# Graph-network layer: gathers as copies with POOL adding them, count blocks copied two units at a time, 92 instead of 100 counted rows

## The reference, cut to what is computed

```python
msg = x[src] + edge_attr                      # 400000 x 64
agg = segment_sum(msg, dst, 12500)
h = relu(agg @ W1 + b1)                       # 64 -> 128
y = x + h @ W2 + b2                           # 128 -> 64
out = (y - mean(y)) / sqrt(var(y) + 1e-5)
```

## Time and profile before

| | us |
|---|---|
| median of 3 runs | 1739.51 (1737.26 to 1742.28) |
| the profiled execution's own time | 1733.04 |
| its span, first to last instruction | 1731.1 |
| PE busy | 1445.1 (83%) |
| DVE busy | 1404.8 (81%) |
| ACT busy | 1182.7 (68%) |
| POOL busy | 1053.7 (61%) |

### The profile page before, as it was taken

The page is one execution under the profiler, slowest core; times in us unless marked ns, Lnnn a source line. Parts: engine busy times, 40 slices in busy tenths (PEclk is TensorE's granted clock), DMA queues, the critical chain, the costliest instruction groups (busy, mean ns, idle before and its releaser), DMA issues.

```text
span 1731.1 us, 49895 instructions
## 1 busy us (share of the span) xinstructions
PE 1445.1 (83%) x19203; PEld 1248.4 (72%) x19204; DVE 1404.8 (81%) x2881; ACT 1182.7 (68%) x2314; POOL 1053.7 (61%) x749
## 2 busy tenths in 40 slices
PE   1357777878998988899999999999999888899884
PEld 1246666767887878888888888888887766777653
DVE  5499999989999899998888888888898666766343
...
GB/s 170 138 81 98 100 100 110 97 91 98 103 103 95 98 88 100 106 100 92 88 87 94 93 86 84 100 82 91 86 87 74 79 57 65 57 54 50 14 66 70
DMA packets 219371, 152.99 MB, mean 88 GB/s; under 512 B 128167, under 2 KB 218039, under 8 KB 218791
## 3 DMA queue, kind: packets, MB, share of 16 engines
...
## 4 chain that ended last, share of the span: by engine, by line
PE 42%; DVE 23%; issue 13%; ACT 13%; DVEq 4%; POOL 1%; POOLq 0%; another core or an unknown queue 0%
PE sums_ps L1132 18%; PE counted_ps L1116 14%; ACT counts L724 12%; DVE oh_key L918 9%; DVE oh_lo L914 8%; PE chunk_ps L1100 6%; DVE onehot L875 3%; DVEq L888 2%; PE turn_ps L1144 2%; DVE lists L896 1%; DVE less_b L827 1%; POOL x_parts L642 1%; DVEq L896 1%; PE turn_ps L1072 0%; PE counted_ps L1203 0%
## 5 line engine op out<-in xcount | busy, mean ns | idle before, releaser
L724 ACT CAST counts<-counted_ps 128x392 bf16<-128x392 f32 (+2 forms) x2018 | 1039.5, 607 | 351.8 <-PE counted_ps L1116 295.2
L601 POOL DMA_INDIRECT gmsg<-in_x,idx_t x625 | 965.0, 1544 | 207.8 <-issue 189.9
L1116 PE MATMUL counted_ps<-oh_key,oh_lo 128*128 128x98 bf16 (+2 forms) x5903 | 756.9, 235 | 162.0 <-DVE oh_key L918 89.8
L1132 PE MATMUL sums_ps<-x_parts,counts 128*128 128x193 bf16 (+3 forms) x6272 | 801.7, 251 | 0.1
L1116 PEld LDWEIGHTS counted_ps<-oh_key,oh_lo 128*128 128x128 bf16 x5903 | 427.5, 100 | 300.5 <-DVE oh_key L918 130.2
L1132 PEld LDWEIGHTS sums_ps<-x_parts,counts 128*128 128x128 bf16 (+3 forms) x6272 | 601.2, 120 | 6.9 <-issue 1.1
L914 DVE TENSOR_TENSOR oh_lo<-counted_ps,tables 128x768 bf16<-128x768 f16 (+5 forms) x773 | 508.1, 657 | 102.4 <-PE counted_ps L1116 94.4
L918 DVE TENSOR_TENSOR oh_key<-counted_ps,tables 128x1176 bf16<-128x1176 f16 (+3 forms) x773 | 572.2, 740 | 0.0
L610 POOL DMA_INDIRECT records<-edge_records,run_at x47 | 49.1, 1045 | 363.8 <-DVE run_at L832 362.9
L1100 PE MATMUL chunk_ps<-onehot,cmsg 128*64 128x32 f32 (+1 forms) x5000 | 188.6, 231 | 25.5 <-DVE lists L896 17.3
L1100 PEld LDWEIGHTS chunk_ps<-onehot,cmsg 128*64 128x64 f32 x5000 | 172.7, 146 | 44.5 <-DVE lists L896 25.7
...
## 6 DMA issues: line engine op xcount, KB each, us to landing
cmsg<-in_edge_attr SPq DMA_DIRECT2D x500, 160.0 KB
gmsg<-in_edge_attr SPq DMA_DIRECT2D x125, 160.0 KB
gmsg<-in_x,idx_t POOLq DMA_INDIRECT x625
...
```

The source lines that it names most:

```text
L601: pool.indirect_dma_start(gmsg[:, at * D:(at + 1) * D], None, x, bass.IndirectOffsetOnAxis(ap=idx_t[:, of:of + 1], axis=0), compute_op=ALU ...
L724: nc.scalar.copy(to, ps.rearrange("p (n h) -> p h n", h=HI)).then_inc(unit_kept, 1)
L1116: mm = nc.tensor.matmul(unit_ps[u % BANKS][:, col:col + slot.key_cols], oh_lo[s % RING][:, n * P:(n + 1) * P], oh_key[s % RING][:, n * slo ...
L1132: mm = nc.tensor.matmul(sums_ps[0:n, 0:XC], counts[b % 2][:, h * P:h * P + n], x_parts[:, h * XC:(h + 1) * XC], start=(h == 0), stop=(h == ...
```

## The change

1. Eight rows of five chunks move from counted to gathered: 460 counted and 165 gathered chunks. The plan has 1609 units, 671 slots, 54 blocks and 43 groups instead of 2018, 773, 64 and 47; what goes are the last 102 slots, all of width three.
2. A gather is a plain copy into a tile of its own, `xmsg` (four buffers). Before gather n POOL waits until gather n - 2 has landed. A POOL instruction (`mix`) adds the 128x320 chunk to the edge features in `gmsg`; that of chunk k - 1 stands after the third gather of chunk k. PE waits for the mix, not the gathers. `gmsg` has six buffers instead of ten.
3. Two units of equal size in one block are copied by one ACT instruction (815 copies). They lie in two neighbouring PSUM banks, and two such pairs of banks take turns. The constants that DVE compares with move to another bank, and the products of both pairs of a quad share one bank.
4. The three parts of a block's sums are added by DVE (`add_parts`: a copy and two adds of 64 columns, each waiting for the one before) and no longer by PE. ACT copies the degree column alone. PE turns them with one matmul.
5. The time scale: 7.35 us per gathered chunk instead of 9.4, and a gathered pair is due two chunks later after its gathers than before.

```diff
-CROWS = 100
+CROWS = 92
...
-    FIRST, LAST = 45.0, 20.0 + 9.4 * gathered + 1.4 * groups
+    FIRST, LAST = 45.0, 20.0 + 7.35 * gathered + 1.4 * groups
...
-    pairs = [(20.0 + chunk * (k + 2) + 5.0, "gather", k) for k in range(0, gathered - 1, 2)]
+    pairs = [(20.0 + chunk * (k + 4) + 4.0, "gather", k) for k in range(0, gathered - 1, 2)]
...
-    BANKS = 3
+    EVICTED = []
+    for u, unit in enumerate(UNITS):
+        if EVICTED and len(EVICTED[-1]) == 1 and (UNITS[u - 1].block, UNITS[u - 1].nodes) == (unit.block, unit.nodes):
+            EVICTED[-1].append(u)
+        else:
+            EVICTED.append([u])
...
-    GSLOTS, CSLOTS = 10, 6
+    GSLOTS, XSLOTS, CSLOTS = 6, 4, 6
...
+        ADD_PARTS.setdefault(min(s0 + n + 2, NS), []).append(b)
+        to = min(s0 + n + 3, NS)
...
             def gather(k, j):
-                t = k % GSLOTS
-                if j == 0:
-                    pool.wait_ge(gin[t], 16 * (k // GSLOTS + 1))
+                t = k % XSLOTS
+                if k >= XSLOTS and j == 0:
+                    pool.wait_ge(mixed, (k - XSLOTS + 1))
                 at, of = t * TILES + j, k * TILES + j
-                pool.indirect_dma_start(gmsg[:, at * D:(at + 1) * D], None, x,
-                                        bass.IndirectOffsetOnAxis(ap=idx_t[:, of:of + 1], axis=0),
-                                        compute_op=ALU.add).then_inc(gathered[t], 16)
+                if of >= 2:
+                    landed(of - 2)
+                pool.indirect_dma_start(xmsg[:, at * D:(at + 1) * D], None, x,
+                                        bass.IndirectOffsetOnAxis(ap=idx_t[:, of:of + 1], axis=0)
+                                        ).then_inc(gathered[of % 4], 16)
+
+            def mix(k):
+                s, t = k % GSLOTS, k % XSLOTS
+                pool.wait_ge(gin[s], 16 * (k // GSLOTS + 1))
...
+                to = gmsg[:, s * TILES * D:(s + 1) * TILES * D]
+                nc.gpsimd.tensor_tensor(to, to, xmsg[:, t * TILES * D:(t + 1) * TILES * D], ALU.add).then_inc(mixed, 1)
...
-                nc.scalar.copy(to, ps.rearrange("p (n h) -> p h n", h=HI)).then_inc(unit_kept, 1)
+                nc.scalar.copy(to.rearrange("p h (m n) -> p h m n", m=m),
+                               ps.rearrange("p m (n h) -> p h m n", h=HI)).then_inc(unit_kept, 1)
...
-                nc.scalar.copy(sums[0:n, 0:XC - 1], sums_ps[0:n, 0:XC - 1]).then_inc(sums_copied, 1)
+                nc.scalar.copy(degrees[0:n, b:b + 1], sums_ps[0:n, XC - 1:XC]).then_inc(degrees_kept, 1)
...
+            def add_parts(b):
+                n = BLOCK_ROWS[b]
+                part = lambda k: sums_ps[0:n, k * D:(k + 1) * D]
+                dve.wait_ge(block_summed, b + 1)
+                dve.wait_ge(degrees_kept, b + 1)
+                if b:
+                    dve.wait_ge(sums_turned, b)
+                nc.vector.tensor_copy(sums[0:n, :], part(0)).then_inc(parts_added, 1)
+                dve.wait_ge(parts_added, 2 * b + 1)
+                nc.vector.tensor_tensor(sums[0:n, :], sums[0:n, :], part(1), ALU.add).then_inc(parts_added, 1)
+                dve.wait_ge(parts_added, 2 * b + 2)
+                nc.vector.tensor_tensor(sums[0:n, :], sums[0:n, :], part(2), ALU.add).then_inc(sums_copied, 1)
...
-                if piece.opens and u >= BANKS:
-                    pe.wait_ge(unit_kept, u - BANKS + 1)
...
+                eviction, bank = EVICTION[u]
+                if piece.opens and not bank and eviction >= 2:
+                    pe.wait_ge(unit_kept, eviction - 1)
...
-                for k in range(PARTS):
-                    mm = nc.tensor.matmul(turn_ps[0:D, 256:256 + n], sums[0:n, k * D:(k + 1) * D], ident[0:n, 0:n],
-                                          start=(k == 0), stop=(k == PARTS - 1))
-                mm.then_inc(sums_turned, 1)
+                nc.tensor.matmul(turn_ps[0:D, 256:256 + n], sums[0:n, :], ident[0:n, 0:n], start=True, stop=True).then_inc(sums_turned, 1)
```

107 lines of the change are left out of this document (62 added, 45 removed).

## The result

The changed kernel takes 1800.59 us (median, 1797.9 to 1821.53) against 1739.51: ratio 1.0372, 95% interval 1.0269 to 1.0474. Forecast were 1548 us and a range to 1620. The profiled execution is the slowest of the three, 21 us above the median: 1821.53 us, its span is 1819.4. First the page's busy times, its clock row, and the chain.

A forecast was written before the change was run, and what follows sets the result against it. DVE bounded width one, PE width two, ACT width three; POOL had room. 1733 - 235 + 30 + 15 - 9 + 10 (both lines ending together) + 2 (chunks behind the last slot) = 1546, predicted 1548 us, range 1505 to 1620.

The forecast's parts named there:

- The 102 slots, -235: Last stretch of width three, from 1387 on: its count matmuls, copies and block multiplies go, saving 235 us; tail unchanged.
- Sums, +15: Block sums on DVE: +17 at width one, +6 at width two, -8 for PE's fewer products; together +15 us.
- chunks moved, +30: 17 quads spread over earlier slots: 9 at 2.1 us where DVE limits, 8 at 1.36 where PE does; +30 us.
- PE's relief: Width two: PE loses two of three fp32 products per block, 16 us for 28 blocks; half counted, -8 us.
- Copies, -9: ACT's copy of two units taken as 0.75 us; pays in the 30 remaining slots of width three, -9 us.
- the rival of the banks: PE waits for ACT to free double banks; 0.15 us for each of 448 pairs is +67, 1615 us; chance 0.1.
- POOL, 8.0 us a chunk: Five gathers, two in flight, plus the mix take POOL 8.0 us (7.2 to 9.2); POOL ends at 1415.
- the prediction's own five steps: POOL's time for a chunk's five gathers and mix; a 3.1 us landing gives 8.2 us, 3.6 gives 9.2.
- Slower than before: The wait for the gather two back makes the kernel slower above 9.3 us a chunk, landing about 3.65; chance 0.04.
- the formula: Total time when POOL limits: 91 + 159 chunks at c us each + 52 for record loads + 107 behind.
- the hold-up between POOL's adds and DVE: Rival: each of 165 mixes stops DVE for 0.7 us, up to +116, 1664 us; chance 0.06.
- POOL's pace: Rival: landings of 3.3 us or more make chunks 8.6 to 9.2 us, total 1617 to 1713; chance 0.17.

The follow-up runs named there:

- e1: Changed kernel with the old adding gathers (ten buffers, no wait on one another), old time scale and 100 counted rows again; 1704.06 us, 0.981 of before.
- e17: Changed kernel with three gathers in flight and a 128x16 POOL memset behind each, POOL waiting only for the memset eight gathers ago; 1562.62 us, 0.909 of before.
- e18: Changed kernel, still two in flight, with a 128x16 POOL memset and the wait for it behind each gather; 1769.55 us, 1.029 of before.
- e10: Changed kernel, still two in flight, with a 128x208 POOL memset and the wait for it behind each gather; 1815.29 us, 1.041 of before.
- e3: Changed kernel with three gathers in flight instead of two, nothing else; 2282.21 us, 1.316 of before.

## Why the prediction failed, step by step

**The 102 slots, -235.** Right: they went, 20 us behind the last slot became 27, and the tail stayed 89.

**Sums, +15, and chunks moved, +30.** e1 has the sums without the quads. Its starts of slots 144, 333 and 641 (rows of L941 in DVE's timeline; 367, 775 and 1320 before) are 368, 794 and 1354. Width one grew by 18 us (forecast 17), width two by 14 where I had -2: the DVE adds of that stretch aren't covered, and half of PE's relief was too much. DVE's three instructions take 0.22 us each. With the quads (e17) the stretches are 435 and 573 us; the terms had made 408 + 17 + 19 = 444 and 545 + 11 - 2 = 554 of them. The sum of the two is 10 us off because 9 us too many in the first make up for half of the 19 too few in the second: in part luck.

**Copies, -9.** e1 shows the last 132 slots at 247 us instead of 301, some 54 for 132 slots, so 12 for 30. A copy of two units of width three takes 0.65 us, not 0.75. The check that I had named for the rival of the banks, PE waiting for ACT by more than 60 us, was met (129.7 us in the changed kernel's group of L1164), and yet it wasn't the banks: with the same banks and copies that group waits 30.0 us for ACT in e17 and 31.1 in e18. ACT was late because PE's signals were: it waited 615.6 us for PE's counts.

**POOL, 8.0 us a chunk: the step that failed.** I took the landing time right on average (2.3 to 2.9 us; 2.82 in e18, and 2.66 in the changed kernel, whose events are less complete) and priced the wait from its mean. In the prediction's own five steps 8.0 us stands for a landing of 3.0, above any mean found. At landings of 2.3 to 2.9 us with starts half of that apart the wait costs nothing only if every landing is like the mean. It isn't: in the changed kernel's timeline 3.20 and 4.16 us stand beside starts that wait for nothing. A wait on the gather two back takes every late landing in full and gives back none of the early ones: 314.4 us over the 825 gathers of the changed kernel, 316.8 in e18, 1.9 us a chunk where I had 0.85. "The wait allows no catching up" stood in the rival; the forecast should have followed it. The chunk took 8.94 us in the changed kernel and 9.67 in e18. How much of the latter is the memset can only be bounded: e10's takes 0.8 us a chunk longer than e18's, and its chunk is 0.26 longer, so the wait swallows most of it, and without it e18's chunk would be between 9.0 and 9.5 (an estimate). The mix took 0.89 us instead of 0.75.

**The rival that came true** is "Slower than before": its mechanism (the wait two back, turning point 9.3 us a chunk, 0.04) is what bounds e18. The changed kernel itself ends slower with a chunk of 8.94, which by the formula gives 91 + 159 x 8.94 + 52 + 107 = 1671. With the 153.7 us that POOL waits for DVE's searches it is 1825, near the 1821.5 of the profiled execution. So the rest has a second cause: what makes DVE late.

**What no step had.** The hold. It was in none of the rivals: the nearest, the hold-up between POOL's adds and DVE, is refuted by one-hots of 737 ns and by e17, which has all 165 mixes. Its share in the changed kernel can't be read from one run. With a chunk of 8.94 to 9.5 us the formula gives 1671 to 1760 us for a changed kernel without it, so it would have cost between 40 and 130. That is argued: the changed kernel itself wasn't run on a chip without lag. e18, which was, lost to the kernel before as well (1.029), by the wait and the memset. On chip 0 three in flight alone made it far worse (e3), since then the gathers stand 1.25 us apart throughout.

**The signs I had named.** One-hots of 0.74 us spoke against the hold-up, rightly. Gathers were 8.94/5 = 1.8 us apart, more than the 1.7 that I had named for POOL's pace, but no wait of PE for mixes showed, and POOL still waited 153.7 us for DVE instead of under 60: a pattern that fitted none of the cases.

**The whole.** Without both losses the sum nearly holds: e17 ran at 1562.6, by its ratio 0.9085 x 1739.5 = 1580 us, 2% over 1548 and at the upper edge of the forecast's own case (1530 to 1580). But e17 has three in flight and ran on chip 14. What it would take on a chip with lag, nobody measured.
